# Banded attention on one Trainium2 core: window weights and bf16 copies from VectorE to GpSimd, rows of maxima from GpSimd's queue, exponentials 1024 wide

## What is computed

```python
scores = q @ k.T / 4                                  # per head, 1024 x 1024
scores = exp(scores - max(scores, axis=-1))
scores = where(-32 <= j - i <= 31, scores, 0)         # band of 64
weights = softmax(scores, axis=-1)
x = layernorm(x + (weights @ v) @ Wo)
```

## Time and profile before

| | us |
|---|---|
| median of 3 runs (lowest, highest) | 2668.9 (2658.05, 2669.55) |
| the profiled execution's own time | 2644.6 |
| its span | 2642.8 |
| banded attention and first norm in that span | about 0 to 1525 |

### The profile page before, as it was taken

One profiled execution on the slowest core, in us unless ns is written; L12 is line 12 of the kernel. 1 busy time (PEld: TensorE's weight loads), 2 busy tenths in 40 slices (PEclk: granted clock), 3 DMA queues, 4 the chain that ended last, 5 costly groups with the idle time before them and its releaser, 6 DMA issues. The chain is left out here.

```text
span 2642.8 us, 46194 instructions
## 1 busy us (share of the span) xinstructions
PE 2100.6 (79%) x13533; PEld 1602.7 (61%) x13533; DVE 1811.0 (69%) x4451; ACT 1392.7 (53%) x2671; POOL 659.4 (25%) x920
## 2 busy tenths in 40 slices
PE   4779888788788898887888668356468848999998
PEld 2345556455555555564555657346467748999997
DVE  3667788778787787787968335536558745777775
ACT  3557667757666676676756212124246533444442
POOL 3110111101111111111100035555521135556511
PEclk8878888989888888898978555667679879999999
DMA  4624643565346435543470081699977742333311
GB/s 72 94 47 67 111 56 62 88 94 70 64 73 111 54 59 94 83 63 70 68 111 18 17 259 70 212 380 341 287 253 248 231 151 84 88 98 100 97 53 39
DMA packets 230094, 306.36 MB, mean 116 GB/s; under 512 B 44445, under 2 KB 145866, under 8 KB 229450
## 3 DMA queue, kind: packets, MB, share of 16 engines
q1 hardware_dynamic: 186746, 199.14, 37.5%
q0 software_dynamic: 22784, 67.13, 7.9%
q10 hardware_dynamic: 20304, 36.97, 3.7%
HBM read 129.33 MB, written 92.27 MB: 84 GB/s over the span
## 5 line engine op out<-in xcount | busy, mean ns | idle before, releaser
L724 DVE CUSTOM_DVE_ANT_0 above<-p_half,above 128x512 f32<-128x512 f32 x1024 | 691.3, 684 | 305.6 <-issue 248.1
L615 ACT ACTIVATE above<-p_diff 128x512 f32<-128x512 f32 x1024 | 599.4, 600 | 269.4 <-PE p_diff L529 267.6
L529 PE MATMUL p_diff<-d_stack,q_stack 96*128 96x512 bf16 x1024 | 433.3, 426 | 127.0 <-ACT above L615 96.0
L533 PE MATMUL p_half<-k_stack,q_stack 96*128 96x512 bf16 x1024 | 431.8, 422 | 31.0 <-DVE row_max L724 27.2
L558 PEld LDWEIGHTS p_pv<-v_win,w_win 128*128 128x128 f32 x2048 | 312.0, 225 | 78.0 <-DVE w_win L758 52.6
L558 PE MATMUL p_pv<-v_win,w_win 128*128 128x34 f32 x2048 | 307.6, 302 | 14.5 <-DVE w_win L758 13.0
L529 PEld LDWEIGHTS p_diff<-d_stack,q_stack 96*128 96x128 bf16 x1024 | 127.0, 125 | 285.3 <-ACT above L615 206.4
L1170 POOL DMA_INDIRECT raw<-sorted_y,place x192 | 206.2, 1074 | 238.5 <-DMA sorted_y<-y_tile 182.9
L641 ACT ACTIVATE p_win<-p_win 128x512 f32<-128x512 f32 x256 | 150.3, 589 | 181.5 <-PE p_win L545 179.9
L421 POOL TENSOR_TENSOR att<-total,inv 128x128 f32<-128x128 f32 x128 | 48.9, 404 | 759.2 <-DVE inv L750 759.2
L1492 ACT ACTIVATE pt_hi<-p_one 128x512 fp32r<-128x512 f32 x128 | 69.6, 595 | 259.6 <-PE p_one L1352 243.9
(11 more groups left out here) (217 smaller groups left out, 4857.1 us busy)
## 6 DMA issues: line engine op xcount, KB each, us to landing
x_tile<-sorted_x SPq DMA_DIRECT2D x141, 256.0 KB
sorted_y<-y_tile ACTq DMA_DIRECT2D x141, 256.0 KB
q_stack<-q_parts SPq DMA_DIRECT2D x256, 96.0 KB, 3.1
k_stack<-k_parts SPq DMA_DIRECT2D x256, 96.0 KB, 3.7
x_in<-in_L_attn_x SPq DMA_DIRECT2D x16, 1024.0 KB, 5.5
x_rows<-x POOLq DMA_DIRECT2D x16, 1024.0 KB
sorted_x<-zeros SPq DMA_DIRECT2D x51, 256.0 KB
d_stack<-d_parts SPq DMA_DIRECT2D x256, 48.0 KB, 3.7
```

The costliest lines, as they stand in the source:

```text
L529: nc.tensor.matmul(p_diff[s % 2][:], qs, d_stack[0:SPLIT_ROWS, h, :], start=True, stop=True).then_inc(s_diff, 1)
L533: nc.tensor.matmul(p_half[s % 2][:], qs, k_stack[g][0:SPLIT_ROWS, h, HALO + S // 2:HALO + S], start=True, stop=True).then_inc(s_half, 1)
L615: nc.scalar.activation(above[:, s % 4], p_diff[s % 2][:], ACT.Relu).then_inc(s_above, 1)
L724: nc.vector.tensor_tensor_reduce(out=above[:, s % 4], in0=p_half[s % 2][:], in1=above[:, s % 4], scale=1.0, scalar=-3.0e38, op0=ALU.add, o ...
```

## The change

- The three transfers of the rows of maxima move from SP's stream to POOL's, right behind the job m that makes the parts.
- The two exponentials are one 1024-wide instruction each, at lags 10 and 11. The second writes to `w_win` in SBUF rather than back to PSUM.
- The window weights move from DVE (two fused instructions of 512 columns, from PSUM) to POOL: one subtraction of 1 and one product with the window, each over 1024 columns in SBUF, at lag 12.
- The copies of bf16 parts move from DVE to POOL, behind the low part.
- `p_win` of the next head waits for the second exponential rather than for the weights, and both halves of the product with the values wait for the whole of the weights.

```diff
-EXP_LAGS = 10, 11, 12, 13
-WEIGHT_LAGS = 13, 14
+EXP_LAGS = 10, 11
+WEIGHT_LAG = 12
 PV_LAGS = 15, 16
...
 (sync, at the start of a unit)
-                    wait_alone(sp, s_mparts, u)
-                    for part in range(3):
-                        row = SPLIT_ROWS + part
-                        sp.dma_start(q_stack[1 - g][row:row + 1, :, :],
-                                     m_parts[:, part, :]).then_inc(s_mrow, 16)
...
 (gpsimd, job m)
+                            pool.wait_ge(s_mparts, u)
+                            wait(pool, s_win, GH * (u - 2))
+                            alone(pool)
+                            for part in range(3):
+                                row = SPLIT_ROWS + part
+                                pool.dma_start(q_stack[1 - g][row:row + 1, :, :],
+                                               m_parts[:, part, :]).then_inc(s_mrow, 16)
...
 (gpsimd, jobs q, k, d)
                             nc.gpsimd.tensor_tensor(parts[:, low, cols], rest[:], parts[:, 2, cols],
                                                     ALU.subtract).then_inc(s_parts, 1)
+                            copy, of = (0, 1) if kind == "q" else (3, 2)
+                            nc.gpsimd.tensor_copy(parts[:, copy, cols], parts[:, of, cols]).then_inc(s_twice, 1)
+                    for w, o, h in late(b, g, s, WEIGHT_LAG):
+                        weights(GH * w + h, h)
...
+            def weights(k, h):
+                wait_alone(pool, s_e2, k + 1)
+                nc.gpsimd.tensor_scalar(w_win[:, h % 2], w_win[:, h % 2], -1.0, None, ALU.add).then_inc(s_less, 1)
+                wait_alone(pool, s_less, k + 1)
+                nc.gpsimd.tensor_tensor(
+                    w_win[:, h % 2].rearrange("p (i j) -> p i j", j=WIN),
+                    w_win[:, h % 2].rearrange("p (i j) -> p i j", j=WIN),
+                    window[:].unsqueeze(1).to_broadcast([P, NBLK, WIN]), ALU.mult).then_inc(s_ww, 1)
...
 (tensor)
-                wait(pe, s_ww, 2 * k)
+                wait(pe, s_e2, k)
...
-                pe.wait_ge(s_ww, 2 * k + part + 1)
+                if part == 0:
+                    pe.wait_ge(s_ww, k + 1)
...
 (scalar)
+                    act.wait_ge(s_e1, k + 1)
+                    wait(act, s_pv, k - 1)
+                    nc.scalar.activation(w_win[:, h % 2], p_win[:], ACT.Exp).then_inc(s_e2, 1)
...
 (vector)
-                            nc.vector.tensor_copy(parts[:, copy, cols], parts[:, of, cols]).then_inc(s_twice, 1)
-                    for n in (0, 1):
-                        for w, o, hh in late(b, g, s, WEIGHT_LAGS[n]):
-                            weights(GH * w + hh, hh, n)
...
-                nc.vector.scalar_tensor_tensor(
-                    w_win[:, h % 2, cols].rearrange("p (i j) -> p i j", j=WIN),
-                    p_win[:, cols].rearrange("p (i j) -> p i j", j=WIN), 1.0,
-                    window[:].unsqueeze(1).to_broadcast([P, NBLK // 2, WIN]),
-                    ALU.subtract, ALU.mult).then_inc(s_ww, 1)
```

More of the change, by code:

```diff
@@ L188, in window_attention @@
         s_e2 = sem("second_exp")
+        s_less = sem("window_exp_less_one")
         s_ww = sem("window_weights")
@@ L265, in unit @@
                     wait_alone(sp, s_const, 17)
-                if not isinstance(b, int) or 1 <= u <= 2 * B:
-                    wait_alone(sp, s_mparts, u)
-                    for part in range(3):
-                        row = SPLIT_ROWS + part
-                        sp.dma_start(q_stack[1 - g][row:row + 1, :, :],
-                                     m_parts[:, part, :]).then_inc(s_mrow, 16)
                 if g == 0 and has(b, -1, 0):
@@ L628, in unit, with exponential @@
                                                  ACT.Copy).then_inc(s_mid, 1)
-                    for n in range(4):
+                    for n in (0, 1):
                         for w, o, h in late(b, g, s, EXP_LAGS[n]):
-                            exponential(GH * w + h, n // 2, n % 2)
-            def exponential(k, again, bank):
-                cols = slice(512 * bank, 512 * bank + 512)
+                            exponential(GH * w + h, h, n)
+            def exponential(k, h, again):
                 if again:
-                    act.wait_ge(s_e1, 2 * k + bank + 1)
-                    nc.scalar.activation(p_win[:, cols], p_win[:, cols], ACT.Exp).then_inc(s_e2, 1)
+                    act.wait_ge(s_e1, k + 1)
+                    wait(act, s_pv, k - 1)
+                    nc.scalar.activation(w_win[:, h % 2], p_win[:], ACT.Exp).then_inc(s_e2, 1)
                 else:
                     act.wait_ge(s_win, k + 1)
-                    nc.scalar.activation(p_win[:, cols], p_win[:, cols], ACT.Exp, scale=DH ** -0.5).then_inc(s_e1, 1)
+                    nc.scalar.activation(p_win[:], p_win[:], ACT.Exp, scale=DH ** -0.5).then_inc(s_e1, 1)
             batches(act, unit)
```

## The result

| | us |
|---|---|
| before, median of 4 runs | 2666.7 |
| after, median of 4 runs (lowest, highest) | 3313.2 (3311.2, 3322.4) |
| ratio after / before, with its 95% interval | 1.244 (1.240 to 1.248) |
| span of the profiled execution, before and after | 2642.8 and 3320.7 |
| last normalisation of the first stage begins at, before and after | 1523.3 and 2190.9 |

The change makes the kernel 24% slower, 647 us. The forecast was 2854, range 2729 to 2975. The sign was right, the size was off by a factor of 3.5: 185 us were forecast. Of the 678 us of span, 668 lie in the first stage.

A forecast was written before the change was run, and what follows sets the result against it. Each head was taken as one chain in which PE waits for POOL's weights: +79 us at full clock and +106 for the clock, +185 on 2644.6, or 2854 us on the runs' scale; range 2729 to 2975.

The forecast's parts named there:

- The mechanism and its place: Between two `p_win` starts, PE's in-order product with the values waits for POOL's weights: plain head 10.3 us against 10.0.
- The queueing: Weights on POOL stand behind other jobs: 3.4 us more in q1 and k1 heads, about 2.9 more behind job m.
- The rows of maxima: Issued from POOL, they leave 7 us earlier, so all of PE's 62.6 us of waiting may go.
- The product on POOL: The two-input product of the window weights on POOL takes 2.15 to 2.3 us for 1024 columns.
- The maxima on DVE: DVE's maxima, never above 0.694 us in 1024 instances before, should not suffer from POOL's new work.
- The price of the subtraction: POOL's one-input subtraction over 1024 columns was taken as 1.1 us, between 0.957 and 2.2.
- The clock: With 26% of the time at 1.2 GHz, a chain 3.4 us longer there costs +106 us over 120 heads.
- The queue behind the pair: On POOL, `att` of a pair, 2 x 0.38 us, precedes the weights every second head: 0.4 us on average.
- The tail: In the tail without scores, `p_win` no longer waits for weights, 1.43 us in each of 7 heads: -7 us.
- The exponentials and the copies: Wide exponentials on ACT booked at nothing; five copies a unit of 0.59 us leave DVE, also booked at nothing.
- DVE relief wins: Rival: with POOL's pair under 2.5 us or PE arriving later, the chain would not bind: -126, 2543 us; 8%.
- POOL is dearer: Rival: subtraction up to 2.2 us, or port waits, adds 0.8 us in 120 heads: 2950 us; 15%.

The follow-up runs named there:

- a_late: The changed kernel with the product with the values four steps later, totals and pairs later and job V2 moved ahead of T0: 2615.1 us, ratio to before 1.000.
- a_nosub: The changed kernel without the subtraction of 1 on POOL, so the weights lack that term: 2911.1 us, ratio to before 1.092.
- a_warm8: The changed kernel with eight unused 128-column products on PE ahead of its wait for the weights in each head: 3177.5 us, ratio to before 1.214.

## Why the prediction was wrong in size

The steps that held:
- The mechanism and its place. PE's in-order product waits for POOL in nearly every head (119 waits, 452 us), and nothing passes it. a_late shows it without taking work away.
- The queueing. From the end of the second exponential to the subtraction I had 0.05 for a plain head and 3.4 more behind q1 and k1; measured, in all and on average, 0.16, and 2.9 to 3.3. Behind m I had 2.9 more, measured 3.8 and 4.3 in all. There two errors of mine nearly cancel: the three transfers took 1.7 us rather than 2.85, but the job m begins after the end of the second exponential (0.7 us in one head, 1.4 in another) and not 0.9 before. Moving the weights ahead gave back 156 us.
- The rows of maxima: PE's wait of 62.6 went, to 3.6.
- The product on POOL: 2.15 to 2.3 against 2.34. Of the two rows that gave the slope only the 128-column one is a product; the 512-column one subtracts two inputs and writes bf16. The Trainium skill ("GPSIMD Engine Reference", section 3.1) gives 4497 ns for an f32 add of two inputs over 2048 columns; half of it, an estimate of 2.25, lies within 4% of the 2.34.
- The maxima on DVE were not slowed by POOL.

The steps that failed, largest first:
- **The price of the subtraction.** "so I take 1.1", between 0.957 and 2.2; it measured 2.775, above the upper end. No row showed a subtraction of a constant, and I bounded it from above by the product's price per column, as though one input could not cost more than two. In the chain the error is 1.7 us a head, about 215 us over 128 heads, and a_nosub shows that it is paid in full: 2.92 us removed from each head gave 407 us. With the product's own 0.2 and the hop, the pair is 1.92 us a head too short in my sum, 246 us.
- **The clock.** "At the same 26%: +106"; it was 60% of the time at 1.2 GHz. By my own 3.4 us a head that is 0.34 x 3.4 x 120 = 139 us more. My upper case was 45%, and my range went only to 40%. The reason stood in my text: new waits of some us in three heads of each unit. With the dearer subtraction they stand in nearly all of them (119 waits in 128 heads), so the two errors are one: the longer the wait, the slower the work behind it. a_warm8 shows at least 101 us of it.
- **The queue behind the pair.** I booked 0.4 us on average for `att`. In the g=1 head of O0 the subtraction began 3.2 us after the exponential on average, 3.95 in the one shown: POOL's pair waits for DVE's reciprocal, which stands behind a job's sum and statistics on DVE, and the weights stand behind the pair. On DVE and POOL (start, duration) this reads

```profile
1002.81 0.69 DVE L711 TENSOR_TENSOR x_in<-p_job,x_in 128x512 f32<-128x512 f32 x1
1003.53 0.75 DVE L717 BATCH_NORM_STATS2 stats<-x_in 128x6 f32<-128x256 f32 x2
1004.20 0.37 DVE L721 BATCH_NORM_AGGREGATE mean_var<-stats 128x2 f32<-128x6 f32 x2
1004.49 0.22 DVE L754 RECIPROCAL inv<-total 128x16 f32<-128x16 f32 x1
...
1004.79 0.76 POOL L426 TENSOR_TENSOR att<-total,inv 128x128 f32<-128x128 f32 x2 [7.75 <-DVE inv L754]
1005.52 2.77 POOL L439 TENSOR_SCALAR w_win<-w_win 128x1024 f32<-128x1024 f32 x1
```

  The second exponential had ended at 1001.57, 4 us before. With the first piece of the chain (3.97 against 3.55) this is 0.8 us a head, some 90 us.
- **The tail.** I booked -7 since `p_win` no longer waits. There the subtraction and product fill POOL: from 2110 to 2150 us it is busy 34 of 40 us and a head takes 6.2 us, from 5.9. There was no gain.
- **The exponentials and the copies**, each booked at nothing: +1.0% and -1.3%. They nearly cancel, which was luck; neither was nothing.

The first three sum to 475 us; the measured loss exceeds the forecast one by 461. The pieces are means of one execution, so the agreement is no finer than some tens of us. The clock's share is the least certain: 139 is my own price at the measured clock, while the last piece of the table, in which most of it should lie, is 1.36 us a head over the forecast, 163 us.

The rivals: *DVE relief wins* asked that POOL's pair take under 2.5 us, and it took 5.1. *POOL is dearer* was the right one at 15%, priced at +0.8 us a head; it needed +1.9, and the clock's answer to it on top.

## What to carry to other kernels

Work moved to an idle engine costs its latency, not its throughput, when an in-order engine waits for it: before the move, find the waiting instruction, count the steps between producer and consumer, and either move the consumer by as much or leave the work where it is. Here the same work cost 24% with three steps of room and, against the kernel before, nothing with seven. It gained nothing either: the fastest kernel leaves the weights on DVE and moves only the rows and the copies, and with the weights on DVE the later product and the moved job cost 4%. An instruction whose price no row shows should be measured alone before it is put into a chain; its bound from above is not that of a seemingly heavier one. And where PE gets new waits, book its lower clock with them, and check each queue that the moved work joins for waits that have nothing to do with it.

## What the runs showed of the hardware that I had not expected

- GpSimd's subtraction of a constant, in place, 128x1024 f32, took 2.775 us (2.759 to 2.941), 2.7 ns a column. Its product of two inputs of that size took 2.344, and a one-input bf16 copy of 512 columns 0.61 (1.2 ns a column).
- Three small transfers issued back to back from GpSimd's queue occupied it for 1.68 us, 0.56 each, where the nearest row had 0.95.
- Unused work on PE paid: eight products more in each head, and 101 us less, by a granted clock of 0.81 rather than 0.70.
- DVE's normalisation (SBUF to SBUF, 128x256) took longer beside POOL: 0.41 us at the median in all kernels, but up to 1.23 after and up to 3.25 in a_nosub, from 0.66 before. Where POOL executed nothing beside it, it never took more than 0.415 in these three traces (133 instances). The one of 3.25, from 657.65, ended 0.15 us after POOL's product of 658.40 to 660.75:

```profile
L710 DVE TENSOR_SCALAR x_in<-x_in,mean_var,rstd x64: 395/408/658, 393.2 to 1523.3; 128x256 f32<-128x256 f32 x64
L725 DVE TENSOR_SCALAR x_in<-x_in,mean_var,rstd x64: 396/410/1227, 512.1 to 2190.9; 128x256 f32<-128x256 f32 x64
L723 DVE TENSOR_SCALAR x_in<-x_in,mean_var,rstd x64: 397/409/3250, 436.0 to 1783.9; 128x256 f32<-128x256 f32 x64
```

  This fits the exclusive port pair that the Trainium skill describes ("SBUF — State Buffer", section "Who interferes with whom"). In all it is 4 us of DVE time after, and 15 in a_nosub.
